# The transposes of the context in a perceiver block are split into halves of 64 keys: the upper half of one group and the lower half of the group behind it alternate

## What is computed

```python
x = x + _L0_xattn_ref(_layernorm(x, axis=-1), ctx_1024, W, b)
x = x + _L0_attn_ref(_layernorm(x, axis=-1), ...)   # linear attention and a feed forward part
x = x + _L0_ffn_ref(_layernorm(x, axis=-1), ...)    # mixture of 8 experts, 2 per token

def _L0_xattn_ref(proj_p, proj_q, W, b):
    trans_q = jnp.einsum('bqh,oh->bqo', proj_q, W) + b
    att_weights = jnp.einsum('bph,bqh->bpq', proj_p, trans_q)
    att_norm = jax.nn.softmax(att_weights, axis=-1)
    att_vec = jnp.einsum('bpq,bqh->bph', att_norm, proj_q)
    return jax.nn.relu(jnp.einsum('bph,oh->bpo', att_vec, W) + b)
```

## Time and profile before

| | |
|---|---|
| median of 3 runs | 670.28 us (668.91 to 671.87) |
| the profiled execution | 669.52 us, of which the span is 666.9 us |
| granted TensorE clock | 0.991 of full speed on average, 1.00 in the loop over the groups |
| TensorE, matmuls | 637.5 us busy, 96% of the span |
| VectorE, ScalarE, GpSimd | 414.5, 371.1 and 245.4 us busy |
| L1405, the transposes of the context | 384 instructions, 57.7 us busy |

### The profile page before, as it was taken

The page is one execution under the profiler, slowest core; times in us unless marked ns, Lnnn a source line. Parts: engine busy times, 40 slices in busy tenths (PEclk is TensorE's granted clock), DMA queues, the critical chain, the costliest instruction groups (busy, mean ns, idle before and its releaser), DMA issues.

```text
span 666.9 us, 10258 instructions
## 1 busy us (share of the span) xinstructions
PE 637.5 (96%) x3720; PEld 525.0 (79%) x3721; DVE 414.5 (62%) x691; ACT 371.1 (56%) x523; POOL 245.4 (37%) x170
## 2 busy tenths in 40 slices
PE   8989999999989999889999999699999999999994
PEld 8867888888867888767888887577888888888883
DVE  7775767658667455567794446661882735753766
ACT  4589998979963344431332443322882736745750
POOL 4059986879883132250000050160022020220233
PEclk9999999999999999999999999789999999999999
DMA  9515544452222413230265962138696573991915
GB/s 327 209 64 198 198 159 166 139 169 96 93 80 71 188 63 128 94 99 31 70 246 157 408 235 77 54 126 300 232 374 228 164 276 118 348 377 45 354 69 184
DMA packets 51846, 116.98 MB, mean 175 GB/s; under 512 B 5208, under 2 KB 5208, under 8 KB 48736
## 3 DMA queue, kind: packets, MB, share of 16 engines
q1 hardware_dynamic: 47360, 106.51, 45.5%
q10 hardware_dynamic: 3168, 5.77, 2.6%
q0 software_dynamic: 1280, 4.20, 1.9%
HBM read 102.31 MB, written 14.16 MB: 175 GB/s over the span
## 4 chain that ended last, share of the span: by engine, by line
PE 78%; DVE 7%; issue 5%; POOL 4%; ACT 4%; DMA 1%; SPq 0%; DVEq 0%; ACTq 0%; POOLq 0%
PE bank L1391 19%; PE bank L1392 18%; PE bank L1393 18%; PE bank L1405 5%; PE bank L1456 3%; POOL nat_lo L478 3%; PE bank L1457 2%; PE bank L1424 2%; PE bank L1425 2%; POOL slots_x L538 1%; PE bank L1819 1%; ACT nat_hi L595 1%; PE bank L1441 1%; PE bank L1632 1%; ACT ct_hi L562 1%
## 5 line engine op out<-in xcount | busy, mean ns | idle before, releaser
L478 POOL TENSOR_TENSOR nat_lo<-raw,nat_hi 128x512 fp32r<-128x512 f32 x104 | 136.2, 1347 | 42.3 <-ACT nat_hi L595 42.1
L526 POOL TENSOR_TENSOR e_lo<-e_raw,e_hi 128x2048 fp32r<-128x2048 f32 x9 | 41.6, 4620 | 221.5 <-ACT e_hi L751 221.5
L871 DVE TENSOR_TENSOR ct_lo<-bank,ct_hi 128x512 fp32r<-128x512 f32 x96 | 65.9, 689 | 33.3 <-ACT ct_hi L562 32.5
L1391 PE MATMUL bank<-w_hi,turned 128*128 128x512 f32 x176 | 70.1, 398 | 1.5 <-DVE turned L1309 1.4
L1393 PE MATMUL bank<-w_hi,turned 128*128 128x512 f32 x176 | 68.7, 391 | 0.0
L1392 PE MATMUL bank<-w_lo,turned 128*128 128x512 f32 x176 | 68.7, 391 | 0.0
L595 ACT ACTIVATE nat_hi<-raw 128x512 fp32r<-128x512 f32 x104 | 64.7, 630 | 0.0
L562 ACT ACTIVATE ct_hi<-bank 128x512 fp32r<-128x512 f32 x96 | 56.9, 596 | 9.0 <-PE bank L1405 6.8
L1391 PE MATMUL bank<-e_hi,turned 128*128 128x512 f32 x144 | 59.0, 409 | 1.5 <-issue 1.5
L1405 PE MATMUL bank<-ident,raw 128*128 128x128 f32 x384 | 57.7, 273 | 0.3
L1392 PE MATMUL bank<-e_lo,turned 128*128 128x512 f32 x144 | 56.9, 395 | 0.0
(11 more groups left out here) (257 smaller groups left out, 1426.2 us busy)
## 6 DMA issues: line engine op xcount, KB each, us to landing
raw<-in_ctx_dram SPq DMA_DIRECT2D x24, 1024.0 KB, 5.0
w_raw<-in_L_ffn_w_dram SPq DMA_DIRECT2D x24, 1024.0 KB, 5.3
e_raw<-in_L_ffn_wo_dram SPq DMA_DIRECT2D x16, 1024.0 KB, 8.0
w_raw<-in_L_attn_w_dram SPq DMA_DIRECT2D x8, 1024.0 KB, 5.2
e_raw<-in_L_ffn_w_dram SPq DMA_DIRECT2D x8, 1024.0 KB, 7.8
slots_x<-zeros SPq DMA_DIRECT2D x1, 4096.0 KB, 15.9
slots_y<-zeros SPq DMA_DIRECT2D x1, 3840.0 KB, 25.6
vectors<-slots_x ACTq DMA_DIRECT2D x11, 256.0 KB, 5.0
```

The costliest lines, as they stand in the source:

```text
L478: nc.gpsimd.tensor_tensor(nat_lo[:, j, :], raw[b % 2][:, j, :], nat_hi[:, j, :].bitcast(f32), ALU.subtract).then_inc(nat_lo_ready, 1)
L526: nc.gpsimd.tensor_tensor(e_lo[j][:, :, :], e_raw[j][:, :, :], e_hi[j][:, :, :].bitcast(f32), ALU.subtract).then_inc(e_lo_ready[j], 1)
L871: nc.vector.tensor_tensor(ct_lo[:, n % CR, :], src, ct_hi[:, n % CR, :].bitcast(f32), ALU.subtract).then_inc(t_lo, 1)
L1391: nc.tensor.matmul(dst, lh, rh, start=first and k == 0, stop=False)
```

## The change

Each transpose of 128x128 becomes two: `half_turned(n, i, 0)` takes keys 0 to 63 of a block, in rows 0 to 63 of the array, to columns 0 to 63 of its quarter of the bank, and `half_turned(n, i, 1)` keys 64 to 127, in rows 64 to 127, to the other 64 columns. `context_turned(n)` now issues the upper halves of group n and the lower halves of group n - 1 in turns. The two lie in different banks and in different rows of the array. A group is therefore complete one turn later, and `split_upto` moves the work of ScalarE and VectorE on it back by one turn, except at the end. Group 12 is turned as before, behind the lower halves of group 11. Group 0 has upper halves alone, as no lower halves are left from the group before it.

```diff
+        def split_upto(s):
+            return turned_upto(s) - (turned_upto(s) < NG_ALL)
...
-            for n in range(3):
+            for n in range(2):
                 upper_context(n)
             for m in range(1, KD):
                 upper_WT(m - 1)
                 upper_pw(m)
-                upper_context(2 + m)
+                upper_context(1 + m)
...
-                for n in range(turned_upto(s - 1) if s else 6, turned_upto(s)):
+                for n in range(split_upto(s - 1) if s else 5, split_upto(s)):
                     upper_context(n)
...
+            def half_turned(n, i, r):
+                b, g = n // G, n % G
+                own = slice(S * r, S * (r + 1))
+                return nc.tensor.transpose(TB[n % 3][:, i * P + S * r:i * P + S * (r + 1)],
+                                           raw[b % 2][own, CH * (g // CH) + i, (g % CH) * P:(g % CH + 1) * P], ident[own, own])
...
                 b, g = n // G, n % G
+                upper_rows_, lower_rows_ = g < G - 1, n >= 1 and (n - 1) % G < G - 1
...
-                if g < G - 1:
-                    for i in range(CH):
-                        mm = nc.tensor.transpose(TB[n % 3][:, i * P:(i + 1) * P],
-                                                 raw[b % 2][:, CH * (g // CH) + i, (g % CH) * P:(g % CH + 1) * P], ident[:, :])
-                else:
+                if lower_rows_:
+                    pe.wait_ge(t_half, n - (n - 1) // G)
+                for i in range(CH):
+                    if upper_rows_:
+                        up_ = half_turned(n, i, 0)
+                    if lower_rows_:
+                        low_ = half_turned(n - 1, i, 1)
+                if upper_rows_:
+                    up_.then_inc(t_half, 1)
+                if lower_rows_:
+                    low_.then_inc(t_done, 1)
+                if g == G - 1:
                     for k in range(KD):
                         mm = nc.tensor.transpose(TB[n % 3][:, k * P:k * P + REMP], raw[b % 2][0:REMP, FULL, k * P:(k + 1) * P],
                                                  ident[0:REMP, 0:REMP])
-                mm.then_inc(t_done, 1)
+                    mm.then_inc(t_done, 1)
```

More of the change, by code:

```diff
@@ L224, in perceiver_block @@
         pb_done, pb_ready = sem("pb_done"), sem("pb_ready")
-        t_done, t_hi, t_lo = sem("t_done"), sem("t_hi"), sem("t_lo")
+        t_half, t_done, t_hi, t_lo = sem("t_half"), sem("t_done"), sem("t_hi"), sem("t_lo")
         s_step, s_low, s_ready = sem("s_step"), sem("s_low"), sem("s_ready")
@@ L980, in _ @@
                 lower_pw(m)
-                lower_context(2 + m)
+                lower_context(1 + m)
             lower_WT(KD - 1)
```

## The result

The changed kernel takes 682.86 us (median of 4 runs, 682.43 to 683.66) against 669.62 us (4 runs), 1.0193 times as long, with a 95% interval of 1.0173 to 1.0213: 13 us slower, where 11 were forecast. The span of the profiled execution went from 666.9 to 680.6 us.

A forecast was written before the change was run, and what follows sets the result against it. TensorE was taken to bound the kernel (78% of the span). +0.2 us ahead of 28 us, +0.7 to 54 and +10.2 to 178 made +11, so 681 us; the forecast's own range was 675 to 688, the wider one 672 to 699.

The forecast's parts named there:

- The way in and out, 0.34 us: On TensorE, going from the whole array to a row half and back costs 0.34 us per place.
- Eight halves in 0.25 us: In a turn of the context, upper and lower halves run side by side, 0.031 us per half, eight in 0.25 us.
- the rival of serial loads: Weight loads of the two row halves follow one another at 0.063 us per half: about 699 us; chance 18%.
- +0.15 per turn, +0.59 at group 12, -0.34 at the softmax: TensorE's change per turn of eight halves, per turn of group 12, and where L1441 follows a turn, in us.
- +10.2: From 54 to 178 us: 72 turns, about 6 of group 12 and 12 places with L1441 add 10.2 us.
- The stretch ahead of 54 us: Loop's early part: +0.2 us ahead of 28 us, +0.7 from 28 to 54, TensorE's idle time covering most.
- I cost it at nothing: ScalarE and VectorE copies one turn later add nothing; without the longer steps, 4 us in all.
- The wait on `t_half`: TensorE waits for its own instruction of a step before: costs nothing.
- The end: Behind 178 us nothing changes but the start; a longer loop moves GpSimd's eleven subtractions back whole.
- The rival of the hidden drain: Half loads slip ahead under whole-array products, so only the gain is left: about 662 us; chance 10%.

The follow-up runs named there:

- the last experiment: Kernel before with whole transposes, but the softmax's own transposes (L1441) read two rows of zeros more, 66 rows by 66 columns: 667.66 us against 670.59, 0.9958.

## Why the prediction was right, and where it was not

**The way in and out, 0.34 us: right.** A step of 1.52 us less 0.92 for the products and 0.25 for the halves leaves 0.35. The kernel with one half more has it by itself, and the last experiment takes it away where it was before the change. That it is a drain of the array is the reading of the Trainium skill, TensorEngine Tiling (Array Packing), section Key Properties, as cited in the prediction. The rows show that nothing is loaded ahead, and that the weight side is idle for 0.37 us (I had expected 0.17) without a reason that the profile knows. The prediction read the way out from a product that starts 0.33 ahead of the next, "not 0.23"; a turn of whole transposes has 0.32 in that place. The price is right because it came from whole steps.

**Eight halves in 0.25 us: right,** and the loads of 128 columns don't stand in each other's way; the rival of serial loads is out with a step of 1.52 and not 1.76. The picture was too narrow: I tied the gain to the alternation, and four and four in sequence do as well.

**+0.15 per turn, +0.59 at group 12, -0.34 at the softmax: right to a few hundredths.** 83.35 - 81.83 is 1.52 us, 0.16 more than before; the step at group 12 is 81.83 - 80.07 = 1.76, where the kernel before has 1.23 (73.61 to 74.84): 0.53 more. One batch in which no query vectors are turned, 81.83 to 103.46, takes 21.63 us against 19.91 before (the same groups stand at 74.84 and 94.75 there). The difference is 1.72; the terms give 12 x 0.15 + 0.59 - 2 x 0.34 = 1.71. For the whole stretch +10.2 was worked out and 9.05 measured; between groups 26 and 103 lie 5 turns of group 12 and not 6, which makes it 9.7. The terms leave no room for waits for `ct_lo` in that batch: the 3.3 us that the later copies cost alone are covered by the longer steps, as argued. The weight loads do wait for `ct_lo` ahead of 11 turns between 54 and 194 us, 0.4 us at most, about as long as the way in holds them anyway.

**The stretch ahead of 54 us: the step that failed.** I gave it +0.2 and +0.7 us, and it lost 5.8 from the first turn to group 26. The step read "cover for most of it; I take +0.7, between nothing and 3.5", and of ScalarE and VectorE "I cost it at nothing". The cover was thin: TensorE's waits of more than 0.15 us in this stretch went from 2.8 to 1.5 us, so 1.3 at most was covered. The longer turns, by the terms above, are 21 x 0.15 + 2 x 0.59 - 2 x 0.34 = 3.7 us. The later copies alone cost 3.4, with a fall of the clock in it, and the clock cost at least 1.7. With 1.3 covered this adds up to 7.5 and not 5.8, so the parts overlap. No run has the halves without the later copies, and how the 5.8 us divide stays open. The run with halves from the third batch shows that this stretch holds all of the loss that was not foreseen.

**The wait on `t_half`: not nothing where turns stand together.** I took it for a wait on an instruction of a step before. In the first three turns it is one of the turn just before: from the first turn to group 3 it is 4.78 us (14.83 to 19.61) instead of 4.49 (14.88 to 19.37), 0.3 more, where I had 0.2 less. This is small here, and it is what two turns at once ran into.

**The end: nearly as foreseen.** I said that a longer loop moves the tail back whole, and up to the last product of the first layer it moved by 14.5 of 14.8 us. The other 0.8 us by which the span is shorter lie behind it, in layers that the change leaves alone. That part took 468.1 us here and 468.9 before, and from 468.1 to 472.3 in the traces of the experiments, so 0.8 us is no finding.

So 11 us forecast were 10.2 + 0.9, and the 13.7 of the span are 9.05 + 5.7 - 1.1: the loop's middle was right by its mechanism, but that the total is close is partly luck, as misses of opposite sign met in it.

The rival of the hidden drain is out: the weights of a row half are not loaded under a product over all rows, and the step is 1.52 us and not 1.17. What stays open is why the clock fell at 43.9 us. Ahead of it TensorE had waited for 0.96 us (up to 42.88). The kernel before waits for 1.2 us in the same place, and is busy for only 2.88 of the 4.00 us from 44 on, without a fall. It fell with the halves in sequence, with two turns at once, and with whole transposes and later copies. It did not with one more instruction per turn, whole or half, with eight in one row half, or with halves from the third batch.

Halves of one group side by side in one bank, which would need no later copies, were not tried.

## What to carry to other kernels

Small products side by side in parts of TensorE's array pay only when enough of them stand together: here the way in and out costs 0.34 us, and a turn saved 0.19. Look at a place that already does it, subtract the instructions' own spacing from the distance between the neighbours, and what is left is the price per visit; then ask whether the few that are there can be widened to the whole array, which won 0.4% here.

Where a schedule has an engine waiting, don't count its idle time as cover for a change that also delays what it waits for: the delay alone cost 3.4 us in such a stretch here. And a semaphore that an engine sets for itself is free only when something else stands in between: back to back it took what the second turn was meant to save.

## What the runs showed of the hardware that was not expected

- Each row half of the array takes its instructions on its own: four upper and four lower halves in sequence are as fast as alternating ones (0.48 and 0.46 us for eight from first start to last end), while eight in one row half take 0.71.
- Transposes with 66 rows go without the way in and out that those with 64 rows need: six of them cost 0.44 us, 0.06 more than their own spacing of 0.063 each, where five with 64 rows cost 0.65, 0.34 more than theirs.
- The granted clock was 0.50 from 43.9 to 54.1 us, after 3.9 us in which TensorE was busy for 2.94; the kernel before was busy for 2.95 of the 4.00 us from 40 on and 2.88 of the next 4.00, and kept 1.00.
